# Four more x tiles of the first batch transposed by DMA in f16 halves instead of by TensorE

## The chip, the cores and the metric

The kernel runs on one core of one Trainium2 chip. The metric is the device time of one execution in microseconds (us). All times below are of that one core. The engines are TensorE (PE), VectorE (DVE), ScalarE (ACT), GpSimd (POOL) and SyncE (SP), which here only issues DMAs.

## The reference

```python
def reference(x, Wq, bq, Wk, bk, Wv, bv, Wo, bo, ffn_w, ffn_scale, ffn_bias):   # x: (8, 1024, 512) f32
    xn = layernorm(x)                                  # eps 1e-5
    q, k, v = (heads(xn @ W.T + b) for ...)            # 16 heads of 32
    scores = q @ k.T / sqrt(32)
    im = arange(1024) % 256
    scores = where(im[:, None] >= im[None, :], scores, -1e30)
    s = merge(softmax(scores) @ v) @ Wo.T + bo
    w = where(ffn_w >= 0, 1, -1)
    g = silu(clip((xn @ w.T) * ffn_scale + ffn_bias, -100, 100))
    return x + s * g
```

## The kernel before, in words

**Layout.** Each of the 8 batches has 1024 rows. They are cut into 8 tiles of 128 rows x 512 columns, so there are 64 tiles; tile i is tile i % 8 of batch i // 8. Every product needs the normalised x transposed: `xT[b % 2]` holds it as two f16 halves, a high one (`xTh`) and a low one (`xTl`, what rounding to f16 left over). A product with a weight runs three matmuls for each of 4 blocks of the contraction: high x high, high x low, low x high. The weights are split into the same two halves (`wh_*`, `wl_*`) by ACT and DVE.

**Two ways to transpose x.** Batch 0 takes the short way: PE transposes the f32 tile against an identity into a PSUM bank `pS` (`transpose_x` on PE, L491, semaphore `s_xt`). ACT copies the bank to `xTh` (`take_xt` on ACT, L725, `s_xh`), and DVE subtracts to make `xTl` (`take_xt` on DVE, L972, `s_xl`). The other batches split first: ACT writes the high half of tile i to `HL[k % 2]` (`split_x` on ACT, L717, `s_hi`), DVE writes the low half beside it (`split_x` on DVE, L965, `s_lo`), and SP issues one DMA transpose of both halves into `xT` (`transpose_x` on SP, L1231, semaphores `s_xd[k % 2]`). There are two `HL` buffers, so ACT's copy k waits until transpose k - 2 has landed.

**Where the first tiles lie.** x tiles 0 to 3 load into `xs`, 4 and 5 into `xr`, 6 and 7 into `On`. ACT normalises the even tiles and POOL the odd ones. The projection of Q and K of head group 0 comes as four products of 12 matmuls: (q, first half), (k, first half), (q, second half), (k, second half), called qk 0 to 3 below. The first two need tiles 0 to 3, the last two also tiles 4 to 7. ACT and DVE take each into `sg` (`stage_qk`, L735 and L981). Then copies from `sg` to `QK` follow by DMA: for each half six from SP (L1277) and six from ACT (`place_first`, L748). The V product of tile 0 (L535) follows on PE.

**What sets the order.** Nothing is scheduled at run time. Every engine merges its strands by due times in an abstract unit (`in_time`), and runs the merged list in order; an instruction that waits holds everything behind it on its engine. `wish` gives the due times of the x tiles, and `FIRST` = -84.67 is that of tile 0. `S_RING` hands out the three `pS` banks to score chunks and to the x tiles that PE transposes.

Two lists are timed by hand: `keep_busy` puts 36 matmuls with no use for the result in the first 16 us, 30 of them from the start and 6 behind the transpose of tile 3; `load_weights` on SP issues the loads of the weights as q0, k0, v, q1, k1, q2, k2 in the first 19 us.

Of the kernel before, what the change touches and what calls it, by code (L numbers as in the profile page):

```python
# [23 lines left out]
NSLOT = 6  # L24
NXS = 4
NPS = 3

# [110 lines left out]
def wish(kind, a, b):  # L138
    if kind == "x" and a == 0:
        return FIRST + (0.0, 0.11, 1.3, 1.35, 9.0, 9.23, 9.77, 9.91)[b]  # L140
    if kind == "x":
# [41 lines left out]
def past(kind, a, b=0):  # L183
# [6 lines left out]
S_RING = sorted([(at_s(i), "s", i) for i in range(len(S_TILES))] +  # L190
                [(wish("x", *divmod(i, NT)), "x", i) for i in range(NT)])
T_RING = sorted([(at_t(i), "t", i) for i in range(len(T_TILES))] + [(at_sums(n), "sm", n) for n in range(NU) if n not in ROW_AT])
# [72 lines left out]
def build(nc, x, wqT, wkT, wvT, woT, wfT, bqk_in, bvc_in, bo_in, fsc, fbi, idf, mqk, zrow, out):  # L265
    ctx = ExitStack()
    with ctx:
# [141 lines left out]
        def x_stands(b, t):  # L409

            if b == 0:
                return (s_xh, t + 1), (s_xl, t + 1)
            k = NT * (b - 1) + t
            return tuple((s_xd[j % 2], 16 * (j // 2 + 1)) for j in (k - 1, k) if j >= 0)
# [66 lines left out]
        def _(e):  # L481
# [9 lines left out]
            def transpose_x():  # L491
                for b in range(1):
                    for t in range(NT):
                        yield at("x", b, t)
                        i = b * NT + t
                        ln.wait_ge(s_id, 16)
                        ln.wait_ge(*row_done(i))
                        ln.wait_ge(*s_bank_free("x", i))
                        for c in range(4):
                            ins = e.transpose(s_bank("x", i)[:, c * P:(c + 1) * P],  # L500
                                              x_tile(i)[:, c * P:(c + 1) * P], identf[:, :])
                        ins.then_inc(s_xt, 1)
# [197 lines left out]
        def _(e):  # L700
# [16 lines left out]
            def split_x():  # L717
                for k in range(NTILE - NT):
                    i = NT + k
                    yield at("x", *divmod(i, NT)) - 1.9  # L720
# [4 lines left out]
            def take_xt():  # L725
                for b in range(1):
                    for t in range(NT):
                        yield past("x", b, t) + -0.02
# [80 lines left out]
            def take_outputs():  # L809
                for n in range(NU - 1):  # L810
                    yield at_pv(n, 4 * (n % NQS) + 3) + 0.59
                    if n < 2:
                        ln.wait_ge(s_xt, NT)
                    ln.wait_ge(s_oh, n - 1)
# [19 lines left out]
            def gates():  # L834
                for i in range(NTILE):
# [4 lines left out]
                    else:  # L840
                        ln.wait_ge(s_lo, NTILE - NT)
                        ln.wait_ge(s_f, i - NT + 1)
# [8 lines left out]
        def _(e):  # L851
# [113 lines left out]
            def split_x():  # L965
                for k in range(NTILE - NT):
                    i = NT + k
                    yield at("x", *divmod(i, NT)) - 0.83
                    ln.wait_ge(s_hi, k + 1)
                    e.tensor_tensor(HL[k % 2][:, 1, :], x_tile(i), HL[k % 2][:, 0, :], ALU.subtract).then_inc(s_lo, 1)  # L970

            def take_xt():  # L972
                for b in range(1):
                    for t in range(NT):
                        yield past("x", b, t) + 0.53
# [240 lines left out]
        def _(e):  # L1216
            ln = Line(e)

            def load_x():
                for i in range(NTILE):  # L1220
                    if i < NT:
                        yield (-119 if i < 4 else -117) + 0.1 * i
                    else:
# [3 lines left out]
                        else:  # L1227
                            ln.wait_ge(s_lo, i - NXS - NT + 1)
                    e.dma_start(x_tile(i), x_view[i // NT, i % NT]).then_inc(x_here(i)[0], 16)

            def transpose_x():  # L1231
                for k in range(NTILE - NT):
                    b, t = divmod(NT + k, NT)
                    yield at("x", b, t)
# [72 lines left out]
            def reload_x():  # L1307
                for i in range(NTILE - NT):
                    yield max(at("f", *divmod(i, NT)), past("o", *divmod(i - 2, NT)) + 3 if i > 1 else -99)
                    ln.wait_ge(s_xt, NT)  # L1310
                    ln.wait_ge(s_o[i % 2], 16 * (i // 2))
# [63 lines left out]
```

## Time and profile before

| | |
|---|---|
| median of 3 runs | 1741.29 us (1740.87, 1741.29, 1746.29) |
| the profiled execution, its own time | 1742.41 us |
| its span, first to last instruction | 1740.6 us |
| PE busy | 1676.8 us, 96% |
| DVE, ACT, POOL busy | 77%, 68%, 70% |
| granted TensorE clock, mean | 0.992 |

The span is what the trace can divide up; some 2 us of the execution's time lie around it. A clock of 1.00 is TensorE's full 2.4 GHz, 0.50 is 1.2 GHz. In the timeline the entries ACTq and SPq are DMA issues by the queue of that engine.

### The profile page before, as it was taken

What the parts mean: (1) busy time and instruction counts of PE and PEld (TensorE: products, weight loads), DVE (VectorE), ACT (ScalarE), POOL (GpSimd) and SP (SyncE); (2) the same over time, 40 slices, a digit from 0 to 9 for tenths busy, and PEclk for the clock granted to TensorE, in tenths of its full rate; (3) what the DMA queues carried; (4) which work ended last, traced back from release to release, by engine and by line L of the source; (5) the groups of instructions that cost most, each with busy time, mean ns of one, the idle gap of its engine ahead of it and who ended that gap; (6) DMA issues with size and microseconds to landing.
All of it is one profiled execution on the core that took longest, in us unless ns stands there. A gap on an engine that the chain in (4) does not pass through costs nothing.

```text
span 1740.6 us, 34003 instructions
## 1 busy us (share of the span) xinstructions
PE 1676.8 (96%) x11652; PEld 778.6 (45%) x11652; DVE 1342.8 (77%) x2620; ACT 1182.6 (68%) x2798; POOL 1222.8 (70%) x1210
## 2 busy tenths in 40 slices
PE   8989999999999999999999999999999999999978
PEld 3433444444444444444444444444444444444423
DVE  6888778787787976888777877778778787687872
ACT  4566777667667766677756777656777667667784
POOL 0077757786777768777588775888757786667773
PEclk9999999999999999999999999999999999999989
DMA  7313312243123421234122331224312242122111
GB/s 209 108 38 81 73 41 59 80 98 80 38 66 82 104 63 44 74 81 110 38 66 65 101 85 37 74 63 111 73 41 59 80 98 56 38 67 70 44 50 49
DMA packets 185038, 126.09 MB, mean 72 GB/s; under 512 B 106912, under 2 KB 159264, under 8 KB 184416
## 3 DMA queue, kind: packets, MB, share of 16 engines
q1 hardware_dynamic: 183904, 123.13, 28.2%
q8 instruction: 92, 1.51, 0.4%
q10 hardware_dynamic: 960, 0.79, 0.2%
q14 instruction: 82, 0.67, 0.1%
HBM read 41.50 MB, written 17.05 MB: 34 GB/s over the span
## 4 chain that ended last, share of the span: by engine, by line
PE 83%; ACT 10%; DVE 5%; issue 2%; ACTq 0%; DMA 0%; POOL 0%; SPq 0%; DVEq 0%
PE pJ L488 29%; PE pO L692 15%; PE pS L649 11%; PE pT L673 10%; ACT pS L802 4%; PE pT L669 3%; PE pJ L580 3%; PE pJ L581 3%; PE pJ L584 3%; PE pS L652 3%; ACT PT L790 2%; DVE mx L1002 2%; PE pT L633 2%; ACT acc L790 1%; ACT HL L723 1%
## 5 line engine op out<-in xcount | busy, mean ns | idle before, releaser
L1002 DVE TENSOR_REDUCE mx<-pS 128x1 f32<-128x512 f32 (+3 forms) x1216 | 782.7, 657 | 295.3 <-PE pS L649 178.3
L790 ACT ACTIVATE PT<-pT 128x512 f32<-128x512 f32 (+1 forms) x1092 | 630.3, 588 | 444.0 <-PE pT L673 362.0
L1178 POOL TENSOR_TENSOR acc<-acc,PT 128x512 f32<-128x512 f32 x620 | 762.1, 1262 | 34.4 <-PE pO L692 34.4
L649 PE MATMUL pS<-QK 96*128 96x512 f16 (+3 forms) x1280 | 392.1, 319 | 22.5 <-ACT pS L802 15.5
L673 PE MATMUL pT<-QK 97*128 97x512 f16 (+3 forms) x1280 | 393.6, 318 | 8.2 <-ACT acc L790 7.1
L802 ACT ACTIVATE pS<-pS,a 128x384 f32<-128x384 f32 (+3 forms) x512 | 270.8, 534 | 11.6 <-DVE a L1017 11.5
L692 PE MATMUL pO<-PT,V 128*32 128x512 f32 (+3 forms) x2824 | 264.7, 489 | 0.0
L649 PEld LDWEIGHTS pS<-QK 96*128 96x128 f16 x1280 | 124.1, 98 | 175.1 <-ACT pS L802 46.1
L488 PE MATMUL pJ<-xT,wh_q 128*128 128x512 f16 x512 | 191.0, 380 | 2.2 <-issue 1.7
L488 PE MATMUL pJ<-wh_v,xT 128*128 128x512 f16 x512 | 192.3, 378 | 0.6 <-ACT V L770 0.4
L488 PE MATMUL pJ<-xT,wh_k 128*128 128x512 f16 x512 | 192.7, 379 | 0.0
L652 PE MATMUL pS<-QK 128*128 128x128 f16 x1024 | 180.4, 220 | 11.3 <-DVE mx L1002 10.5
L669 PE MATMUL pT<-QK 128*128 128x128 f16 x1024 | 180.6, 220 | 8.5 <-ACT PT L790 5.7
L673 PEld LDWEIGHTS pT<-QK 97*128 97x128 f16 x1280 | 124.9, 98 | 120.3 <-ACT acc L790 12.6
L1188 POOL TENSOR_TENSOR On<-On,R 128x512 f32<-128x512 f32 x63 | 82.9, 1316 | 122.7 <-DVE R L1081 122.5
L1191 POOL TENSOR_TENSOR Onl<-On,Onh 128x512 f16<-128x512 f32 x63 | 73.2, 1162 | 105.1 <-ACT Onh L827 104.9
L488 PE MATMUL pJ<-wf,xT 128*128 128x512 fp8e4 x512 | 141.9, 378 | 0.0
L692 PEld LDWEIGHTS pO<-PT,V 128*32 128x32 f32 x2824 | 75.5, 110 | 136.6 <-issue 114.8
L669 PEld LDWEIGHTS pT<-QK 128*128 128x128 f16 x1024 | 91.3, 98 | 100.4 <-ACT PT L790 25.5
L652 PEld LDWEIGHTS pS<-QK 128*128 128x128 f16 x1024 | 94.7, 98 | 72.6 <-issue 12.3
L802 ACT ACTIVATION_READ_ACCUMULATOR pS<-pS,a 128x1 f32 x512 | 123.0, 240 | 0.0
L745 ACT ACTIVATE sg<-pJ,bqk 128x512 f16<-128x512 f32 x128 | 90.8, 709 | 45.9 <-PE pJ L488 41.1
(162 smaller groups left out, 2364.1 us busy)
## 6 DMA issues: line engine op xcount, KB each, us to landing
QK<-sg SPq DMA_DIRECT2D x756, 64.0 KB
xs<-in_x SPq DMA_DIRECT2D x60, 256.0 KB, 3.1
xr<-in_x SPq DMA_DIRECT2D x58, 256.0 KB, 3.0
out<-xr SPq DMA_DIRECT2D x58, 256.0 KB, 2.5
QK<-aT SPq DMA_DIRECT2D x256, 1.0 KB, 1.7
rq<-moved SPq DMA_DIRECT2D x132, 2.0 KB, 1.7
QK<-in_x SPq DMA_DIRECT2D x8, 256.0 KB, 3.8
QK<-in_mqk SPq DMA_DIRECT2D x2, 512.0 KB, 9.3
```

Of the source, the lines that this page charges most:

```text
L488: ins = e.matmul(bank(kind, a, b)[:, :], p, q, start=n == 0, stop=n == len(terms) - 1)
L649: ins = e.matmul(s_bank("s", i)[:, base:base + wide], q4[0:96, j, qc], k4[0:96, j, 0:wide], start=True, stop=True)
L652: ins = e.matmul(s_bank("s", i)[:, base + wide:base + width], q4[:, j, qc], k4[:, j, qc], start=True, stop=True)
L669: ins = e.matmul(slot[:, to:to + P], k4[:, j, kc], q4[:, j, q0:q0 + P], start=True, stop=True)
L673: ins = e.matmul(slot[:, to:to + 512 - q0], k4[0:97, j, kc], q4[0:97, j, q0:512], start=True, stop=True)
L692: ins = e.matmul(pO[32 * j:32 * j + 32, 512 - width:512], V[:, s, kb, 32 * j:32 * j + 32], probs, start=kb == 0, stop=kb == nkb - 1)
L745: e.activation(sg[:, 2 * which, cs], bank("qk", gn, o)[:, :], ACT.Identity, bias=bqk[:, which, gn % NG:gn % NG + 1]).then_inc(s_qh, 1)
L790: e.activation(probabilities_at(i), t_bank("t", i)[:, 0:cols], ACT.Exp, scale=SS).then_inc(s_p, 1)
L802: ins = e.activation(scores, scores, ACT.Exp, bias=row_shift(i)[:, c:c + 1], scale=SS, accum_out=rS[:, ROW_AT[n] % 2, part, c:c + 1])
L1002: e.tensor_reduce(mx[:, par, part, :].rearrange("p (j q) -> p j q", q=4)[:, heads[0]:heads[-1] + 1, qi], s_bank("s", i)[:, 0:cols].rearran ...
L1178: e.tensor_tensor(a, a, PT[:, RING_AT[i] % NPT, 0:width * len(heads)].rearrange("p (j q) -> p j q", j=len(heads)), ALU.add).then_inc(s_ap, 1)
L1188: e.tensor_tensor(On[n % 2][:, :], On[n % 2][:, :], R[:, :], ALU.mult).then_inc(s_on, 1)
```

## The change

A new constant `NXP = 4` says how many tiles PE transposes. Tiles 4 to 7 leave the PE strand and the two `take_xt` strands, and enter the strands that split and transpose the other batches: `k` now counts from tile 4. Their due times move from 9.0 ... 9.91 after `FIRST` to 8.0 ... 10.0. Those who waited for all eight PE transposes (`s_xt`) wait for four halvings (`s_lo`).

```diff
+NXP = 4
...
     if kind == "x" and a == 0:
-        return FIRST + (0.0, 0.11, 1.3, 1.35, 9.0, 9.23, 9.77, 9.91)[b]
+        return FIRST + (0.0, 0.11, 1.3, 1.35, 8.0, 8.8, 9.2, 10.0)[b]
...
-                [(wish("x", *divmod(i, NT)), "x", i) for i in range(NT)])
+                [(wish("x", *divmod(i, NT)), "x", i) for i in range(NXP)])
...
         def x_stands(b, t):
-            if b == 0:
+            k = NT * b + t - NXP
+            if k < 0:
                 return (s_xh, t + 1), (s_xl, t + 1)
-            k = NT * (b - 1) + t
             return tuple((s_xd[j % 2], 16 * (j // 2 + 1)) for j in (k - 1, k) if j >= 0)
...
             def transpose_x():
                 for b in range(1):
-                    for t in range(NT):
+                    for t in range(NXP):
                         yield at("x", b, t)
...
             def split_x():
-                for k in range(NTILE - NT):
-                    i = NT + k
+                for k in range(NTILE - NXP):
+                    i = NXP + k
                     yield at("x", *divmod(i, NT)) - 1.9
                     ln.wait_ge(*row_done(i))
                     ln.wait_ge(s_xd[k % 2], 16 * (k // 2))
...
             def take_xt():
                 for b in range(1):
-                    for t in range(NT):
+                    for t in range(NXP):
...
                     if n < 2:
-                        ln.wait_ge(s_xt, NT)
+                        ln.wait_ge(s_lo, NT - NXP)
...
             def split_x():
-                for k in range(NTILE - NT):
-                    i = NT + k
+                for k in range(NTILE - NXP):
+                    i = NXP + k
                     yield at("x", *divmod(i, NT)) - 0.83
                     ln.wait_ge(s_hi, k + 1)
...
             def transpose_x():
-                for k in range(NTILE - NT):
-                    b, t = divmod(NT + k, NT)
+                for k in range(NTILE - NXP):
+                    b, t = divmod(NXP + k, NT)
                     yield at("x", b, t)
                     ln.wait_ge(s_lo, k + 1)
```

The other edits only shift counts by the same four tiles (`load_x`, `reload_x`, `gates`). Behind the places shown here the order of every engine is as before, but for the names of the `pS` banks.

On PE, between product qk 1 (the last matmul with `wl_k`, `wh_k`) and product qk 2 (`wh_q`), there stood before:

```order
L488 MATMUL pJ<-xT,wh_k 128x512
L500 MATMUL pS<-identf,xr 128x128 [waits s_ln]
L500 MATMUL pS<-identf,xr 128x128 [waits s_lz]
L500 MATMUL pS<-identf,On 128x128 [waits s_ln]
L500 MATMUL pS<-identf,On 128x128 [waits s_xl,s_lz]
L488 MATMUL pJ<-xT,wh_q 128x512 [waits s_ql,s_xl,s_xh]
```

and each of the four L500 rows is followed by three more of its kind. With the change there stands at the same place:

```order
L489 MATMUL pJ<-xT,wl_k 128x512
L489 MATMUL pJ<-xT,wh_k 128x512
L489 MATMUL pJ<-xT,wh_q 128x512 [waits s_ql,s_xd1,s_xd0]
L489 MATMUL pJ<-xT,wl_q 128x512
L489 MATMUL pJ<-xT,wh_q 128x512 x2
```

The 16 transposing matmuls are gone, and product qk 2 waits for the landing of the DMA transposes (`s_xd0`, `s_xd1`).

On ACT, from the normalising of tile 6 (`On<-On,ab`) on, there stood before:

```order
L714 ACTIVATE On<-On,ab 128x512 [waits s_la]
L745 ACTIVATE sg<-pJ,bqk 128x512 [waits s_qk]
L731 ACTIVATE xT<-pS 128x4x128 [waits s_xt] x2
L707 ACTIVATE wh_v<-PT 128x512 [waits s_wv]
L731 ACTIVATE xT<-pS 128x4x128 [waits s_xt] x2
L707 ACTIVATE wh_v<-PT 128x512 x3
L758 DMA QK<-sg 32x2x512 [waits s_ql,s_qh,s_mask0]
```

and with the change, from the row ahead of it on:

```order
L724 ACTIVATE HL<-xr 128x512 [waits s_ln]
L715 ACTIVATE On<-On,ab 128x512 [waits s_la]
L724 ACTIVATE HL<-xr 128x512 [waits s_lz]
L724 ACTIVATE HL<-On 128x512 [waits s_xd0,s_ln]
L724 ACTIVATE HL<-On 128x512 [waits s_xd1,s_lz]
L746 ACTIVATE sg<-pJ,bqk 128x512 [waits s_qk]
L708 ACTIVATE wh_v<-PT 128x512 [waits s_wv]
L708 ACTIVATE wh_v<-PT 128x512 x3
L759 DMA QK<-sg 32x2x512 [waits s_ql,s_qh,s_mask0]
```

Four copies into `HL` have taken the place of four copies out of PSUM, two of them wait for a DMA, and the staging of product qk 1 (`sg<-pJ,bqk`), the halving of `wh_v` and the six DMA issues now stand behind these waits. DVE has the same: its four subtractions into `HL` stand ahead of its part in the staging of qk 1.

On SP, behind the load of the last Q and K weights (`PT<-in_wkT`, called k2), there stood before:

```order
L1247 DMA PT<-in_wkT 128x4x256
L1277 DMA QK<-sg 32x2x512 [waits s_ql,s_qh,s_mask0]
L1277 DMA QK<-sg 32x2x512 x5
L1279 DMA QK<-in_zrow 1x2048
L1277 DMA QK<-sg 32x2x512 [waits s_ql,s_qh]
```

and with the change:

```order
L1248 DMA PT<-in_wkT 128x4x256
L1239 DMA_TRANSPOSE xT<-HL 128x8x128 [waits s_lo] x4
L1278 DMA QK<-sg 32x2x512 [waits s_ql,s_qh,s_mask0]
L1278 DMA QK<-sg 32x2x512 x5
L1280 DMA QK<-in_zrow 1x2048
```

Four transposes have come in, behind all the early loads and ahead of the copies from `sg` to `QK`.

## Rows read from the trace of the kernel before

**Rows 1.** The page: span, and the chain that ended last, by engine.

```profile
span 1740.6 us, 34003 instructions
PE 83%; ACT 10%; DVE 5%; issue 2%; ACTq 0%; DMA 0%; POOL 0%; SPq 0%; DVEq 0%
```

**Rows 2.** A stretch: busy PE, PEld, DVE, ACT, POOL; PEclk, DMA share, GB/s.

```profile
400.00:800.00 400.00, 393.26 (x2771) 184.40 (x2769) 313.19 (x596) 269.94 (x623) 306.50 (x304) 1.00 0.29 72
```

**Rows 3.** The chain of waits, 18 to 46 us: start, length, what.

```profile
20.30 0.81 ACT xr L714
...
22.43 0.75 DVE sg L988
...
26.27 5.35 PE pJ L488 x24
31.65 0.69 ACT sg L745
```

**Rows 4.** Timeline of PE: start us, us, engine line op tiles count [idle before].

```profile
21.14 0.38 PE L488 MATMUL pJ<-xT,wh_k 128*128 128x512 f16 x1
...
26.27 0.38 PE L488 MATMUL pJ<-xT,wh_q 128*128 128x512 f16 x1 [1.72 <-issue]
```

**Rows 5.** Timelines of POOL, of the DMA issues of ACT, and of SP.

```profile
21.11 0.77 POOL L1135 TENSOR_SCALAR On<-On,ab 128x512 f32<-128x512 f32 x1
...
33.21 4.12 ACTq L758 DMA_DIRECT2D QK<-sg  x6
...
11.84 4.14 SPq L1247 DMA_DIRECT2D acc<-in_wqT  x1
16.02 2.97 SPq L1247 DMA_DIRECT2D PT<-in_wkT  x1
```

**Rows 6.** L1238, the DMA transposes of the other batches, and their halvings: ns min/median/max.

```profile
L1238 SPq DMA_TRANSPOSE xT<-HL x56: 1230/1256/2361, 140.0 to 1445.7; - x56
DMA to landing us min/median/max: 3.0/3.3/5.5
...
L723 ACT ACTIVATE HL<-xs x56: 618/638/793, 137.8 to 1443.9; 128x512 f16<-128x512 f32 x56
...
L970 DVE TENSOR_TENSOR HL<-xs,HL x56: 676/1151/1775, 138.6 to 1445.0; 128x512 f16<-128x512 f32 x56
```

**Rows 7.** DMA issues from 11 to 19 us; the last number: us to landing.

```profile
acc<-in_wqT SPq DMA_DIRECT2D x1, 512.0 KB, 13.1
PT<-in_wkT SPq DMA_DIRECT2D x1, 512.0 KB, 11.4
```

**Rows 8.** Three stretches, columns as in group 2.

```profile
23.00:25.00 2.00, 0.63 (x4) 0.42 (x4) 2.00 (x5) 1.78 (x4) 0.00 (x0) 1.00 1.08 333
25.00:27.00 2.00, 0.73 (x4) 0.40 (x5) 2.00 (x4) 1.74 (x4) 0.00 (x0) 1.00 0.84 189
...
140.00:145.00 5.00, 4.75 (x28) 1.57 (x30) 3.54 (x8) 5.00 (x13) 1.15 (x1) 1.00 0.48 105
```

**Rows 9.** Timelines of PE and its weight loads: the start, and the longest gap.

```profile
1.48 0.15 PEld L510 LDWEIGHTS pO<-row 128*128 128x128 f16 x1 [0.28 <-issue]
1.91 0.15 PEld L510 LDWEIGHTS pO<-row 128*128 128x128 f16 x1 [0.28 <-issue]
...
4.45 4.42 PEld L510 LDWEIGHTS pO<-row 128*128 128x128 f16 x21 [0.26 <-issue]
...
126.05 0.39 PE L649 MATMUL pS<-QK 96*128 96x256 f16 x1 [4.35 <-ACT pS L802]
```

**Rows 10.** Two stretches behind that gap, columns as in group 2.

```profile
128.00:130.00 2.00, 2.00 (x15) 0.98 (x17) 1.34 (x4) 2.00 (x8) 0.00 (x0) 0.50 0.00 0
130.00:132.00 2.00, 2.00 (x20) 0.42 (x12) 0.38 (x2) 0.59 (x3) 0.00 (x0) 0.82 0.00 0
```

**Rows 11.** Timelines of DVE and of POOL ahead of that gap.

```profile
118.99 4.87 DVE L1037 TENSOR_TENSOR mx<-mx 128x16 f32<-128x16 f32 x1
...
104.28 19.55 POOL L1178 TENSOR_TENSOR acc<-acc,PT 128x512 f32<-128x512 f32 x16
```

More of the change, by code:

```diff
@@ L840, in gates @@
                     else:
-                        ln.wait_ge(s_lo, NTILE - NT)
+                        ln.wait_ge(s_lo, NTILE - NXP)
                         ln.wait_ge(s_f, i - NT + 1)
@@ L973, in take_xt @@
                 for b in range(1):
-                    for t in range(NT):
+                    for t in range(NXP):
                         yield past("x", b, t) + 0.53
@@ L1227, in load_x @@
                         else:
-                            ln.wait_ge(s_lo, i - NXS - NT + 1)
+                            ln.wait_ge(s_lo, i - NXS - NXP + 1)
                     e.dma_start(x_tile(i), x_view[i // NT, i % NT]).then_inc(x_here(i)[0], 16)
             def transpose_x():
-                for k in range(NTILE - NT):
-                    b, t = divmod(NT + k, NT)
+                for k in range(NTILE - NXP):
+                    b, t = divmod(NXP + k, NT)
                     yield at("x", b, t)
@@ L1309, in reload_x @@
                     yield max(at("f", *divmod(i, NT)), past("o", *divmod(i - 2, NT)) + 3 if i > 1 else -99)
-                    ln.wait_ge(s_xt, NT)
+                    ln.wait_ge(s_lo, NT - NXP)
                     ln.wait_ge(s_o[i % 2], 16 * (i // 2))
```

## The prediction

> **What bounds the kernel now.** I read the page first, for the span and the chain that ended last [rows 1]: PE makes 83% of that chain, ACT 10%, DVE 5%, and DMA rounds to nothing. Then a long stretch of the middle [rows 2]: there PE is busy 393 of 400 us, and the other engines keep up. So the middle is a chain of PE work without slack, and its order does not change. All of it depends on the first projections: nothing there is tied to a fixed time, for the loads of later tiles are issued by SP behind the copies of this very start. A delay of the start should therefore reach the end whole, and a gain too.
>
> So I read the start closely. The chain of waits [rows 3] runs from ACT's normalising of tile 4 (20.3 us) over ACT and DVE to product qk 2, which begins at 26.27 us; its 24 matmuls (qk 2 and 3) are on the chain, and then ACT's staging of qk 3. The timeline of PE [rows 4] shows the same from PE's side: qk 1 ends at 21.5, then come the 16 transposes, and qk 2 begins at 26.27. These transposes are PE work, but PE was waiting anyway; what counts is how soon tile 7 stands in `xT`. Call the start of qk 2 S. Before, S = 26.3.
>
> **What the change removes.** 16 small matmuls on PE and four ACT copies and four DVE subtractions out of PSUM. The PE work lies in a gap, so its removal gives nothing by itself. The ACT and DVE work is replaced one for one, by copies of about the same length. Gain: 0.
>
> **What it adds: the way of tile 7 to `xT`.** I walk it with the durations of the other batches' tiles [rows 6]: high half on ACT 0.62 (the shortest; nothing else runs then), low half on DVE 0.68 (the shortest, since POOL is idle after 21.9 [rows 5] and nothing can hold DVE up), 1.25 for SP to issue a transpose, 3.3 from issue to landing (3.0 to 5.5). I allow 0.05 us for each hand-over from engine to engine; this is an estimate from the 0.01 to 0.1 us between rows of the chain.
>
> - Tile 4 is normalised at 21.1 [rows 3]. High half to 21.8, low half to 22.6, issue at 22.65.
> - Tile 5: ACT normalises tile 6 in between (0.7), so the high half is done at 23.1, the low half at 23.9, issue at 23.95.
> - Tiles 6 and 7 need the two `HL` buffers again. ACT therefore waits until the transposes of tiles 4 and 5 have landed.
>
> When do these land? At 22.65 the queue of SP is not empty. The load q2 was issued at 11.84 and k2 at 16.02 [rows 5], and they land 13.1 and 11.4 us later [rows 7], at 24.9 and 27.4, in the order of issue. The stretches say the same: the DMA engines are fully taken until 25 at 333 GB/s, and still 0.84 until 27 [rows 8]. Both loads are 512 KB, which take 1.5 to 1.6 us at that rate, so without ACT's own copies, which now come later, k2 would be down at about 26.4. I take the transposes to queue behind it. What one costs the DMA engines I get from 140 to 145 us, where one transpose and one 256 KB load ran alone: 0.48 x 5 = 2.4 us of all engines, less 0.85 for the load (262 KB at 333 GB/s, times 1.08) leaves 1.55 [rows 8]. So tile 4 lands at 26.4 + 1.55 = 28.0 and tile 5 at 29.5.
>
> The Trainium skill, page DMA: Bandwidth & Descriptors, section Queues, rings and completion order, says that all DMAs issued by SP use one ring on each DMA engine and are consumed in ring order. By that rule the transposes queue behind k2, as I take them to; a quick landing in spite of the loads would speak against it.
>
> - Tile 6: high half 28.05 to 28.7, low half to 29.4, issue 29.45, landing 32.75.
> - Tile 7: high half 29.55 to 30.2, low half to 30.95, SP free again at 30.7, issue 31.0, landing 34.3.
>
> So S = 34.4, which is 8.1 us later than before.
>
> The Trainium skill has a rule that speaks louder against the change. Its page VectorE: DVE Perf Modes, section The three transpose paths, gives 1309 ns for one 128x128 block of 16-bit numbers by DMA against 390 ns on TensorE. A tile here has eight such blocks; one after another they would be 10.5 us, tile 5 would land at 34.4 and tile 7 at 46.4, and the total would be 22 us. The trace does not bear this out: 56 transposes of this very shape land in 3.3 us [rows 6], so I give it no chance.
>
> **What is queued behind the waits.** On ACT the staging of qk 1 stood at 21.7 and now comes behind the high half of tile 7, at 30.2; DVE's part comes at 31.0. Behind it on ACT stand the halving of `wh_v` (4 x 0.6) and six DMA issues, which took 4.1 us at the other half [rows 5]: 33.3 to 37.5. Next on ACT is the staging of qk 2, which PE finishes 2.75 us after S, at 37.2 or later. So this work fits below the wait and costs nothing; if tile 7 came earlier than about 32.5, it would be what is late next. SP's six copies of the first half come behind the last transpose, from 32.3, and have until some 10 us after S. After S everything repeats at the old distances: the staging of qk 3 at S + 5.4 [rows 3], then the six issues of ACT and the V products. No time is won back there.
>
> **What it adds: a cold TensorE.** PE now has nothing to do from 21.5 to 34.4, 12.9 us. In the trace a gap of 4.35 us ended at 126.05 [rows 9], and behind it the granted clock was 0.50, that is 1.2 GHz, until about 131.3: 0.50 from 128 to 130 and 0.82 from 130 to 132 [rows 10]. This was 5.2 us at half speed, a loss of 2.6 us. At the start of the program the weight loads follow each other in 0.43 us, twice the 0.21 of later, from 1.1 to 4.45 [rows 9]: 3.4 us, a loss of 1.7. I take the mean, 2.1 us. It falls on the 24 matmuls of qk 2 and 3, which are on the chain, so it counts whole.
>
> **The sum.** 8.1 + 2.1 = 10.2 us. The profiled execution had 1742.41 with a span of 1740.6; with the change it would have 1752.6. The median of the runs is 1.1 below that execution, so I predict 1741.3 + 10.2 = 1751.5.
>
> **Bounds.** Low: the transposes don't feel the loads. Tile 4 lands at 25.95, tile 5 at 27.25, tile 7 is issued at 28.75 and lands at 32.05: S + 5.8, and with the smaller loss of clock 7.5. High: k2 lands at 27.4 as before, tile 5 at 30.5, tile 7 is issued at 32.0, and meets the copies from `sg` of SP and ACT that follow on its heels, 5.5 us: 37.5. With the larger loss of clock this is 11.2 + 2.6 = 13.8.
>
> **The rivals.**
> - *No queue.* The low case. For it speaks that a transpose is made of small pieces which could slip in between; against it that the loads land in order. 1749 (5.8 + 2.1 = 7.9). Chance 0.14.
> - *Crowded landing.* The high case, 1755. For it speaks that transposes with other copies behind them took up to 5.5 us [rows 6]; against it that SP issues its copies only 1.25 us later and the DMA engines are otherwise empty by then. Chance 0.12.
> - *Not slower: the stall at 119 us goes.* DVE's small maximum (L1037) took 4.87 us there, and ended just when POOL's 16 additions, back to back since 104.28, were over at 123.83 [rows 11]. PE's gap of 4.35 us and the 2.6 us of clock hang on it, 7.0 us together. If POOL and DVE met otherwise after a shifted start, 10.2 - 7.0 = 3.2 would be left, 1744.5, no measurable change. It decides once DVE reaches L1037 between two of the additions instead of ahead of them. Against it: both engines are shifted by the same start, so they should meet as before. Chance 0.06.
>
> The Trainium skill, page SBUF — State Buffer, section Who interferes with whom, says that a DVE instruction with two inputs in SBUF and a GpSimd instruction that reads SBUF exclude each other; by that rule the stall is a matter of which issues first.
>
> **Chances and range.** The forecast has 0.65, its own range is 1749.5 to 1754; 0.03 is left for what I did not think of. A measurement of this kernel tells about 0.3%, 5.2 us, from no change. The forecast and the first two rivals all lie above 1746.5, that is 0.91 slower; the third rival and half of the rest give 0.07 for the same; 0.02 faster. The range has to hold 8 in 10: I reach from 1747.5, just below the low case, to 1757, above the high case.
>
> **What would show it.** The first matmul of qk 2 near 34.4, waiting for the DMA into `xT`. Transposes issued near 22.7, 24, 29.5 and 31; the first two land 4 to 6 us after their issue, the last two about 3.3. ACT waits for them ahead of its third copy into `HL`. PE's matmuls 0.43 us apart for 3 to 5 us behind S. The staging of qk 3 some 7.5 us after S, and every later row about 10 us later than before, the stall at L1037 included, with PE as busy as before in the middle. The forecast is wrong if S is right but the end moves by another amount (slack in the middle that I don't see), or if the transposes land in another time than their 56 fellows.

## The result, and the profile after

The changed kernel takes 1755.69 us (median of 4 runs, 1754.62 to 1758.49); the kernel before, on the same chip, 1743.79 (4 runs, 1740.87 to 1746.89). The ratio is 1.007, with a 95% interval of 1.0045 to 1.0096: slower, by 11.9 us in the medians, where 10.2 were forecast. The profiled execution took 1755.81 us, its span is 1754.0 and its mean granted clock 0.988.

First the page and a stretch of the middle, to set beside [rows 1, 2]:

```profile
span 1754.0 us, 33979 instructions
PE 81%; ACT 9%; DVE 5%; issue 2%; DMA 1%; SPq 1%; ACTq 0%; DVEq 0%
```

```profile
400.00:800.00 400.00, 394.46 (x2765) 184.60 (x2758) 310.53 (x590) 275.30 (x639) 300.01 (x289) 1.00 0.29 71
```

The middle is as full as it was: PE busy 394 of 400 us. What is new in the chain is 1% DMA. The chain of waits from 20 us on shows where it lies, as against [rows 3]:

```profile
20.11 0.82 ACT xr L715
...
22.84 0.70 DVE HL L971
23.54 0.16 SPq L1239
23.75 4.60 DMA xT<-HL
28.44 0.64 ACT HL L724
29.10 0.70 DVE HL L971
29.80 0.36 SPq L1239
30.21 4.19 DMA xT<-HL
...
34.49 8.05 PE pJ L489 x24
42.57 0.69 ACT sg L746
```

The normalising of tile 4 starts where it did (20.11, before 20.30). Then the end is set by tile 5's halves, its transpose, tile 7's halves in the buffer that this frees, and its transpose: two landings, 8.8 us together, stand on the path. Product qk 2 starts at 34.49 instead of 26.27, and its 24 matmuls take 8.05 us instead of 5.35. 8.2 + 2.7 = 10.9 us: the staging of the first V product, next on ACT, starts at 48.27 where it started at 37.37.

The two sides of the gap, in the timelines of PE (the number in brackets is idle time, with what ended it) and of SP:

```profile
20.95 0.38 PE L489 MATMUL pJ<-xT,wh_k 128*128 128x512 f16 x1
34.49 0.58 PE L489 MATMUL pJ<-xT,wh_q 128*128 128x512 f16 x1 [13.16 <-DMA xT<-HL]
```

```profile
16.05 2.66 SPq L1248 DMA_DIRECT2D PT<-in_wkT  x1
22.33 9.21 SPq L1239 DMA_TRANSPOSE xT<-HL  x4
```

The line of the four transposes, by source, and ACT's timeline, which shows what stands behind its two waits:

```profile
L1239 SPq DMA_TRANSPOSE xT<-HL x4: 1233/1355/2649, 22.3 to 30.2; - x4
...
DMA to landing us min/median/max: 3.2/4.4/5.1
```

```profile
27.55 0.63 ACT L724 ACTIVATE HL<-On 128x512 f16<-128x512 f32 x1 [4.75 <-DMA xT<-HL]
28.44 0.63 ACT L724 ACTIVATE HL<-On 128x512 f16<-128x512 f32 x1 [0.26 <-DMA xT<-HL]
28.97 0.67 ACT L746 ACTIVATE sg<-pJ,bqk 128x512 f16<-128x512 f32 x1
...
30.56 0.70 ACTq L759 DMA_DIRECT2D QK<-sg  x1
...
48.27 1.08 ACT L771 ACTIVATE V<-pJ 128x512 f32<-128x512 f32 x2 [3.97 <-PE pJ L489]
```

In order of tiles 4 to 7 the landings took 5.1, 4.6, 3.2 and 4.2 us from the issue. The first two are over at 27.45 and 28.35. The queue ahead of them is there: k2, issued at 16.05, needed 10.5 us to land, so it was down at 26.5.

The Trainium skill, page DMA: Bandwidth & Descriptors, section Queues, rings and completion order, has SP's DMAs consumed in ring order. By that rule, the trace agrees: the first transpose landed 0.9 us behind the load ahead of it, 5.1 us after its own issue. From the 1309 ns for one block of its page VectorE: DVE Perf Modes, section The three transpose paths, eight blocks one after another are estimated at 10.5 us. The trace does not agree with that: 3.2 us for the least disturbed tile.

The clock, in stretches (the third number from the end is the granted clock, then DMA share and GB/s):

```profile
23.00:25.00 2.00, 0.00 (x0) 0.00 (x0) 0.53 (x1) 0.00 (x0) 0.00 (x0) 1.00 1.77 315
25.00:27.00 2.00, 0.00 (x0) 0.00 (x0) 0.00 (x0) 0.00 (x0) 0.00 (x0) 0.83 0.75 124
27.00:29.00 2.00, 0.00 (x0) 0.00 (x0) 0.69 (x1) 1.19 (x3) 0.00 (x0) 0.50 0.48 108
...
37.00:39.00 2.00, 2.00 (x6) 0.73 (x5) 0.00 (x0) 0.00 (x0) 0.00 (x0) 0.50 0.03 5
39.00:41.00 2.00, 2.00 (x8) 0.78 (x7) 0.47 (x1) 0.69 (x1) 0.00 (x0) 0.75 0.00 0
41.00:43.00 2.00, 2.00 (x11) 0.88 (x9) 0.28 (x1) 0.43 (x1) 0.00 (x0) 1.00 0.00 0
```

With PE idle since 21.3, the clock fell to 1.2 GHz in the stretch from 25 to 27 us and came back in that from 39 to 41, some 5 us after PE had taken up work: 6 matmuls in 2 us, later 11. A mean of 0.75 from 39 to 41 puts its return at 40.0, 5.5 us after S, and the 2.7 us lost are half of that.

And the stall that the third rival spoke of, DVE's small maximum and PE's gap behind it, in the timelines of DVE, POOL and PE; compare [rows 9, 11]:

```profile
129.81 4.88 DVE L1038 TENSOR_TENSOR mx<-mx 128x16 f32<-128x16 f32 x1
```

```profile
115.10 19.56 POOL L1179 TENSOR_TENSOR acc<-acc,PT 128x512 f32<-128x512 f32 x16
```

```profile
136.87 0.40 PE L650 MATMUL pS<-QK 96*128 96x256 f16 x1 [4.36 <-ACT pS L803]
```

Each row stands 10.8 us later than before, and its lengths are the same. Downstream I follow the 63 rows in which ACT takes an attention output out of PSUM (`On<-pO`, L818, before L817), one per unit of work. After against before they are late by 10.86 us (the first, at 94.81), 11.3 (the third, at 146.57), 11.9 (at 614.14), 12.0 (at 1607.52). So what is lost by the first V product is whole at the end, with 1.1 more on the way. Only the last few rows scatter (+10.8 to +13.4). In the last 100 us the granted clock falls to 0.50 at other places in the two executions, which may be why.

### The profile page after: what moved, and what is told of

It is laid out like the page before. It is cut to its first block, busy times and chain, and to the rows that moved or that the text cites. A ratio compares the mean times of both kernels' runs of the same rounds, so it can differ in the third digit from the quotient of the medians.

```text
span 1754.0 us, 33979 instructions
## 1 busy us (share of the span) xinstructions
PE 1679.4 (96%) x11636; PEld 777.8 (44%) x11636; DVE 1343.5 (77%) x2620; ACT 1183.0 (67%) x2798; POOL 1224.2 (70%) x1210
## 3 DMA queue, kind: packets, MB, share of 16 engines
q1 hardware_dynamic: 188128, 124.18, 28.4%
## 4 chain that ended last, share of the span: by engine, by line
PE 81%; ACT 9%; DVE 5%; issue 2%; DMA 1%; SPq 1%; ACTq 0%; DVEq 0%
PE pJ L489 29%; PE pO L693 15%; PE pS L650 10%; PE pT L674 9%; ACT pS L803 3%; PE pT L670 3%; PE pJ L581 3%; PE pJ L582 3%; PE pJ L585 3%; PE pS L653 3%; ACT PT L791 2%; DVE mx L1003 2%; PE pT L634 1%; ACT acc L791 1%; ACT HL L724 1%
```

## The experiments

In the table S is the first useful matmul of qk 2, and V the staging of the first V product; the profiled execution of before has S 26.27, V 37.37. The next two columns say how late V and the take of the 21st output (600 us) are against that execution. L1038 is the length of the stalled maximum (also called L1037 or otherwise, by the kernel). The ratios stand for all runs, the other columns for one execution of each kernel.

| kernel | S | 24 matmuls | V late | 21st late | L1038 | ratio to before, 95% |
|---|---|---|---|---|---|---|
| changed | 34.49 | 8.05 | 10.9 | 11.9 | 4.88 | 1.0045 to 1.0096 |
| e1_warm | 34.66 | 5.35 | 8.4 | 5.6 | 1.07 | 1.0027 to 1.0047 |
| e2_delay | 34.39 | 5.35 | 8.1 | 4.2 | 1.07 | 1.0028 to 1.0064 |
| e3_four | 33.34 | 7.72 | 9.4 | 7.2 | 1.05 | 1.0027 to 1.0061 |
| e4_late | 31.73 | 7.32 | 7.2 | 7.8 | 4.87 | 1.0021 to 1.0047 |
| e5_apart | 32.70 | 7.59 | 8.7 | 8.6 | 4.87 | one run |
| e6_all | 29.85 | 5.34 | 3.3 | 0.1 | 1.06 | 1.0010 to 1.0034 |
| e7_reduce | 26.32 | 5.35 | 0.0 | -0.1 | moved | 0.9994 to 1.0016 |
| e8_six | 30.32 | 7.02 | 5.7 | 5.5 | 4.89 | one run |
| e10_pause_before | 26.88 | 5.35 | 0.6 | 0.8 | 4.88 | 0.9987 to 1.0005 |
| e11_pause_after | 34.44 | 7.44 | 10.2 | 10.3 | 4.87 | 1.0042 to 1.0067 |
| e12_gap_before | 26.05 | 5.36 | -0.2 | -3.9 | 1.07 | 0.9977 to 0.9997 |
| e13_gap_after | 34.47 | 6.68 | 9.5 | 6.0 | 1.08 | 1.0019 to 1.0037 |

**e1_warm: the changed kernel with PE kept busy in the gap.** 56 matmuls more whose result nobody uses.

```diff
-                for when, count in ((-200, 30), (at("x", 0, 3) + 0.1, 6)):
+                for when, count in ((-200, 30), (at("x", 0, 3) + 0.1, 6), (at("qk", 0, 2) - 0.01, 56)):
```

> The changed kernel with 56 matmuls of no use for the result put into PE's gap ahead of product qk 2 (some 12.1 us at 0.215 us each, the gap is 13.5). Theory (late tiles plus a cold TensorE): qk 2 still starts at 34.5 us, since the transposes decide it, but its 24 matmuls with qk 3 take 5.35 us in place of 8.05, the staging of qk 3 begins at 39.9 in place of 42.6, and the whole is 2.7 us below the changed kernel, some 9.2 above the one before. Rival (the clock costs nothing of its own, the loss is all waiting): time as the changed kernel, some 11.9 above the one before.

1751.62 us (10 runs) against 1744.92 (14). A stretch in the gap, and the chain of waits behind S:

```profile
27.00:29.00 2.00, 2.00 (x11) 0.88 (x9) 0.61 (x1) 1.05 (x2) 0.00 (x0) 1.00 0.60 132
```

```profile
34.66 5.35 PE pJ L489 x24
```

The clock stays at 2.4 GHz, the 24 matmuls take 5.35 us again, and V comes 2.54 us sooner. The cold TensorE is a cost of its own. But from 130 us on the profiled execution had made up nearly 3 us more, which no theory of the start explains: its L1038 took 1.07 us and not 4.88. The median is 6.7 us above before, where 9.2 had been expected.

**e2_delay: the kernel before, held up by as much.** It has all eight PE transposes, and 46 idle matmuls behind the last one.

```diff
-                for when, count in ((-200, 30), (at("x", 0, 3) + 0.1, 6)):
+                for when, count in ((-200, 30), (at("x", 0, 3) + 0.1, 6), (at("qk", 0, 2) - 0.01, 46)):
```

> The kernel before with 46 matmuls of no use for the result behind PE's last transpose (9.9 us), so that qk 2 starts at about 34.5 us while nothing else of the change is there: no DMA transpose, no cold TensorE. Theory (a delay of the start reaches the end whole): the take of the first outputs from pO on ACT is 8.2 us later than in the kernel before, and the whole is 8.2 us longer. Rival (the middle has slack and the loss comes from other effects of the change): clearly less than 8.2, say 3 to 5 us.

1754.04 us (4 runs: 1748.69 to 1754.63) against 1744.92: +9.1 for a delay of 8.1 (the interval, 1.0028 to 1.0064, is 4.9 to 11.2 us). A late start without any DMA transpose costs what it is late. The profiled execution was the 1748.69 one; its maximum took 1.07 us and its 21st output was late by 4.2 instead of 8.1.

**e3_four: four buffers.** Tiles 6 and 7 have their halves in `Onl`, which nothing else uses then, so that ACT waits for no landing. DVE and SP take the halves of these tiles from there too.

```diff
+        def halves(k):
+            return Onl[:, k - 2, :].rearrange("p (a d) -> p a d", a=2) if k in (2, 3) else HL[k % 2]
...
-                    ln.wait_ge(s_xd[k % 2], 16 * (k // 2))
-                    e.activation(HL[k % 2][:, 0, :], x_tile(i), ACT.Copy).then_inc(s_hi, 1)
+                    if k > 3:
+                        ln.wait_ge(s_xd[k % 2], 16 * (k // 2))
+                    e.activation(halves(k)[:, 0, :], x_tile(i), ACT.Copy).then_inc(s_hi, 1)
```

> The changed kernel with two more buffers for the halves (tiles 6 and 7 are split into memory that is free until the outputs come), so ACT doesn't wait for the first two transposes to land. Theory (the two buffers and the queue in front of the transposes make the chain): all four are issued by about 29 us and the last lands at 31 to 32, qk 2 starts there, 2.5 to 3.5 us sooner than in the changed kernel, and the whole is as much shorter, some 9 above the one before. Rival (the DMA engines, not the buffers, set the pace: the transposes pile up behind the loads and slow each other): qk 2 starts at 33.5 or later and the whole is within 1 us of the changed kernel.

1752.46 us (4 runs), 7.5 above before where some 9 had been expected. SP's timeline and the chain:

```profile
22.63 3.83 SPq L1243 DMA_TRANSPOSE xT<-HL  x2
26.50 3.19 SPq L1243 DMA_TRANSPOSE xT<-Onl  x2
```

```profile
27.88 5.37 DMA xT<-Onl
33.34 7.72 PE pJ L492 x24
```

The last transpose is issued at 27.88 us instead of 30.21, yet S comes only 1.15 us sooner, between the two expectations and nearer to the rival's 33.5. Without its wait ACT reaches its six small copies at 25.8, in the midst of the transposes, and the last of these takes 5.4 us to land. The buffers are a wait that can be taken away, but the landings behind it grow.

**e4_late: nothing queued ahead.** The loads q2 and k2 are issued behind the first copies from `sg`.

```diff
-                                   ("q2", -111), ("k2", -110.9), ("o", -41), ("f", -40)):
+                                   ("q2", -73.9), ("k2", -73.8), ("o", -41), ("f", -40)):
```

> The changed kernel with the loads q2 and k2 (512 KB each) issued by SP behind the first copies from sg to QK instead of at 12 to 19 us, so the transposes of tiles 4 and 5 meet a shorter queue. Theory (they stand behind the loads): tile 4 lands 3.2 to 3.7 us after its issue in place of 5.1, tile 5 3.5 in place of 4.6, qk 2 starts 1 to 2.5 us sooner than in the changed kernel, and the whole is as much shorter. Rival (a transpose takes its 4 to 5 us for another reason here, such as its first use or its neighbour): landings as before, 5.1 and 4.6, and no change of time.

1751.01 us (5 runs), 6.1 above before. The line of the transposes, and the chain:

```profile
DMA to landing us min/median/max: 3.1/3.2/3.3
```

```profile
23.73 3.13 DMA xT<-HL
...
28.38 3.26 DMA xT<-HL
31.73 7.32 PE pJ L489 x24
```

S comes 2.8 us sooner, more than the 1 to 2.5 expected: the landings fell from 5.1, 4.6, 3.2 and 4.2 to 3.3, 3.1, 3.2 and 3.3. Tile 5 lands 1.5 us sooner (26.86, before the edit 28.35). Another 0.9 is the last landing, 3.26 for 4.19: here the small copies start 0.7 us behind its issue, not 0.35. So not all of the 2.8 is the queue. This is the low case of the prediction made real (S + 5.8 there, + 5.5 here), and the loads ahead are the largest single part of the delay.

**e5_apart: the small copies wait for the last transpose.** ACT's and SP's copies from `sg` of the first half wait until tile 7 has landed (the diff shows ACT's part; SP's is the same).

```diff
                     ln.wait_ge(s_mask[0], 16)
+                    for signal in x_stands(0, 7):
+                        ln.wait_ge(*signal)
                     ln.wait_ge(s_qh, 2 * half + 2)
```

> The changed kernel, in which SP and ACT issue the copies of the first half from sg to QK only after all four transposes have landed. Theory (the last transpose took 4.2 us, against 3.2 for the one before it, because ACT's copies came 0.35 us behind it): the last lands in 3.2, qk 2 starts at 33.5 us in place of 34.5, and the take of V on ACT is 1.0 us sooner than in the changed kernel; the delayed copies are hidden. Rival (the 4.2 has another reason): qk 2 stays at 34.5.

1752.95 us in one run. The line of the transposes, and the chain:

```profile
DMA to landing us min/median/max: 3.1/3.5/4.3
```

```profile
29.48 3.13 DMA xT<-HL
32.70 7.59 PE pJ L489 x24
```

Tile 7 lands in 3.1 us instead of 4.2, which gives 1.0 of the 1.8 us by which S is sooner; the rest is that the first two landed sooner in this execution (4.3 and 3.8), which the edit does not touch. They did so with k2, which was down at 25.8 here and not at 26.5: the first transpose lands 0.9 us behind that load in all seven executions that have it ahead (changed, e1, e3, e5, e8, e11, e13). Copies beside a transpose do hold it up: 4.2 us also in e1, e11 and e13. But in e4_late they started 0.7 us behind the last issue and it landed in 3.3 us, in the changed kernel 0.35 us behind and it took 4.2; how near they must be stays open.

**e6_all: all four edits.** Four buffers, late loads, copies apart, and 36 idle matmuls in the gap. The diff shows the last and the second; the other two stand as in e3_four and e5_apart.

```diff
+                for when, count in ((-200, 30), (at("x", 0, 3) + 0.1, 6), (at("qk", 0, 2) - 0.01, 36)):
...
+                                   ("q2", -73.9), ("k2", -73.8), ("o", -41), ("f", -40)):
```

> The changed kernel with all that was found: two more buffers for the halves, q2 and k2 loaded late, the copies from sg to QK behind the last transpose, and 36 matmuls of no use for the result in PE's gap. Theory (even with every removable cost gone, four transposes of 1.25 us issue and 3.2 us landing behind the halving end later than PE's way): the last transpose lands at 29.5 to 30, qk 2 starts there, 3.5 us later than in the kernel before, and the whole is 3 to 4 us longer than before where the stall of DVE's small maximum is the same in both. Rival (the way by DMA is as good once its waits are gone): qk 2 at or below 27 us and no difference.

1748.3 us (10 runs, 1741.95 to 1751.28) against 1744.21 (23 runs): +4.1. The landings are 3.4, 3.3, 3.3 and 3.2 us, S is 29.85. What I had found to be removable is gone; 3.6 us of the way are left, and the medians show about as much (the profiled execution does not: it has the short stall, and is the fastest of the ten). The way by DMA is longer here than that over PE even with all this out of its way.

**e7_reduce: the stalled maximum in another form.** The kernel before, with the two-input maximum as a reduction of one input into a tensor of its own.

```diff
-                        e.tensor_tensor(mx[:, par, 0, :], mx[:, par, 0, :], mx[:, par, 1, :],
+                        e.tensor_reduce(mm[:, par, :], mx[:, par, :, :].rearrange("p t c -> p c t"), AX.X,
                                         ALU.max).then_inc(s_am, 1)
```

> The kernel before, in which DVE's small maximum (L1037) is a reduction with one input in place of a tensor_tensor with two, into a small tensor of its own; nothing else is changed. Theory (the 4.87 us at 119 us is DVE waiting for POOL, whose additions ran back to back, because both inputs lie in SBUF): the operation takes 0.2 us in every execution, the take of the outputs on ACT behind it is 4.0 us sooner, as in the two runs where the stall fell to 1.07 us, and the median is 3 to 4 us below the kernel before. Rival (the 4.87 us has another reason, such as the fetch of code): the operation still takes 1 to 5 us and the time is the same.

1744.26 us (12 runs) against 1744.21 (23): nothing. DVE's timeline says why:

```profile
118.96 0.18 DVE L1038 TENSOR_REDUCE mm<-mx 128x16 f32<-128x32 f32 x1
119.17 4.67 DVE L1042 TENSOR_SCALAR a<-mm 128x16 f16<-128x16 f32 x1
```

The reduction passes in 0.18 us, and the very next operation, a scaling of 16 numbers per partition with one input, takes over the wait, 4.67 us. The expectation fell: it is not the two-input form alone that waits for POOL. The addition that POOL had running, the 12th of its 16, shows that the reduction went through beside it:

```profile
118.74 1.26 POOL L1179 TENSOR_TENSOR acc<-acc,PT 128x512 f32<-128x512 f32 x1
```

**e8_six: PE transposes six tiles, DMA only two.** Product qk 2 also waits for the two more tiles of PE.

```diff
-NXP = 4
+NXP = 6
...
-        return FIRST + (0.0, 0.11, 1.3, 1.35, 8.0, 8.8, 9.2, 10.0)[b]
+        return FIRST + (0.0, 0.11, 1.3, 1.35, 9.0, 9.23, 9.2, 10.0)[b]
```

> Half of the change: PE transposes tiles 4 and 5 too, only 6 and 7 go by DMA, each with a free buffer. Theory: the two transposes are issued at about 23.5 and 25 us, stand behind k2 and land 4.5 us later, qk 2 starts at 29 to 30 us, 3 us later than before and 5 sooner than in the changed kernel, PE's gap is some 6 us and cold TensorE costs 1 to 2.7; the take of V on ACT comes 4 to 6 us later than before. Rival (each tile costs the same): half of the 8.2 us, qk 2 at 30.4, no sharp difference to the theory; a start of 33 or later would say that the waiting for landed buffers is not what makes the change slow.

1749.88 us in one run. The chain:

```profile
24.30 5.93 DMA xT<-HL
30.32 7.02 PE pJ L489 x24
```

SP issues the two transposes from 22.87 on. One round of landings is left instead of two, and half of the loss: S + 4.05 and 1.67 us of clock make V 5.7 us late. S is 30.32, so that the rival (each tile costs the same, 30.4) is not told from the theory (29 to 30). And the one round is the longest of all (4.9 and 5.9 us), with the queued load ahead and ACT's copies, from 24.2 on, beside it.

**e10_pause_before and e11_pause_after: a wait in POOL's additions.** It was meant to let DVE in. The shifts that its count 1 stands for are made at 72 us, long before, so it never held POOL: in their work the two kernels are those of before and after again.

```diff
                     ln.wait_ge(s_pv, units(n) + 1)
+                    if k == 16:
+                        ln.wait_ge(s_a16, 1)
```

> The kernel before with one wait added on POOL: its 17th addition, at 119.5 us, waits until DVE has made the shifts of unit 1, so that the back-to-back additions leave DVE a gap. Theory (DVE's 4.87 us at 119 us, and the 4.67 that moved to the next operation when the first was made a reduction, are DVE waiting for a gap of POOL): the small maximum takes at most 0.7 us, PE's gap of 4.35 us goes, the take of the outputs behind it is 4.0 us sooner, and the median is 2 to 4 us below the kernel before, less than 4 because some executions of the kernel before have the short stall anyway. Rival (POOL's loss of its place costs as much): stall gone, time the same or longer.

> The changed kernel with the same wait on POOL. The stall is then the same in both kernels and can't blur their difference. Theory (8.2 us later start of qk 2 and 2.7 of cold TensorE, passed on whole): 10.9 us above e10_pause_before at the take of V and at every take of the outputs up to 1600 us, and 10 to 12 us in the median. Rival (the middle takes part of it back, or adds to it beyond the first 140 us): below 9 or above 13.

1743.48 us (11 runs) against 1744.39 (15), and 1753.55 (5 runs). The stall was there in both (4.88 and 4.87 us), so this missed its aim. As a repetition of the main comparison it is worth having: e11 is late against e10 by 9.63 us at V, 9.68 at the first output, 9.75 at the third, 9.5 at the 21st, 9.77 at 1,596 us, and 10.07 in the medians. (S of e10 is 26.88; the clock was at 0.6 from 12 to 16 us of that execution, which may be why.)

**e12_gap_before and e13_gap_after: the wait for the right count.** The last four of POOL's additions now wait until DVE has made the second set of shifts, L1041.

```diff
+                    if k == 16:
+                        ln.wait_ge(s_a16, 2)
```

> As e10_pause_before, with the wait mended: the first wait was for the first of these shifts, which DVE makes at 72 us, so it never held POOL; now POOL's 17th addition waits for the second one, behind the stall at 119 us. Theory (the 4.87 us are DVE waiting for a gap between POOL's additions): the small maximum takes at most 1.1 us, POOL pauses some 0.7 us at 120, PE's gap of 4.35 us goes, the take of the outputs at 135.3 us comes 3.5 to 4.0 us sooner, and the median is 1.5 to 4 us below the kernel before (less than 4, because some executions of it have the short stall anyway). Rival (another reason for the 4.87): it stays, and POOL's pause adds its length.

> The changed kernel with the same wait. Theory: again a short maximum, and against e12_gap_before 10.9 us at the take of V and in the middle, 9.5 to 12 in the median. Rival (the stall at 119 us has part in the difference of the two kernels): the difference of the medians leaves that band.

In e12 the timelines of DVE, POOL and PE, and a stretch behind the place:

```profile
118.68 1.07 DVE L1037 TENSOR_TENSOR mx<-mx 128x16 f32<-128x16 f32 x1
```

```profile
103.96 15.76 POOL L1180 TENSOR_TENSOR acc<-acc,PT 128x512 f32<-128x512 f32 x12
120.04 3.85 POOL L1180 TENSOR_TENSOR acc<-acc,PT 128x384 f32<-128x384 f32 x4 [0.32 <-DVE a L1041]
```

```profile
122.72 0.28 PE L649 MATMUL pS<-QK 96*128 96x256 f16 x1 [1.34 <-ACT pS L802]
```

```profile
124.00:128.00 4.00, 3.07 (x31) 0.95 (x30) 3.97 (x9) 3.26 (x10) 0.00 (x0) 1.00 0.02 1
```

DVE's maximum ends with the addition that is running, PE's gap shrinks from 4.35 to 1.34 us, the clock does not fall, and the third output is taken at 131.30 instead of 135.32, 4.0 us sooner, of which 0.3 were there before the stall. The kernel takes 1741.59 us (11 runs) against 1744.14 (21), ratio 0.9977 to 0.9997: one added wait beats both kernels. Of the eleven profiled executions without it that have the maximum in its old form, four had the short stall anyway; seven elevenths of 3.7 us, 2.4, is my estimate for the medians, and they show 2.6.

Why 3.7 us and not the 7.0 that I had put on the stall? Part of the answer is the stretch above: behind the gap PE is busy only 3.07 of 4 us at full clock, and DVE 3.97, so PE has room there. But the slow clock is not free. e1_warm and e2_delay have the same short stall (1.07 us) and the same gap of PE (1.93 us), and differ in the clock behind it:

```profile
132.00:136.00 4.00, 3.96 (x21) 1.34 (x25) 3.80 (x9) 4.00 (x14) 0.13 (x1) 0.59 0.09 19
```

```profile
132.00:136.00 4.00, 3.66 (x35) 1.41 (x35) 3.96 (x9) 4.00 (x14) 0.00 (x0) 1.00 0.07 12
```

The first is e1, the second e2: PE works on 21 matmuls against 35, at a mean clock of 0.59 against 1.00. From the start of the maximum to the third output e1 takes 13.55 us and e2 12.38. That e1 has the change and e2 not is no reason: in e12 and e13, with the clock full in both, it is 12.62 and 12.63. So the slow clock, 3.4 us at half speed, cost 1.2 us there, and not the whole half, 1.7.

e13 takes 1749.98 us (11 runs), 5.7 below the changed kernel as it was first timed. Against e12 it is late by 9.75 us at V, 9.80 at the first output, 9.75 at the third, 9.94 at the 21st, 9.98 at 1,602 us. The medians are 8.4 apart, below the 9.5 to 12 expected, which was to speak for the rival, that the stall has part in the difference. The runs leave that open: those of e12 span 6.0 us and those of e13 4.6, and the two profiled executions, both with the short stall, are 9.98 apart. At V, too, 10.9 had been expected. The difference there is the clock: 6.68 us for the 24 matmuls in this execution, 7.44 in e11, 8.05 in the changed kernel, with S within 0.05 us in all three.

## Why the prediction was right

**The middle has no slack.** Right, and shown from three sides: e2_delay (8.1 us of pure delay, 8.0 at the first output, +9.1 in the medians), e11 against e10 (9.6 at V, 10.07 at the end), e13 against e12 (9.75 at V, 9.98 at 1,602 us).

**The removal gives nothing.** Right: PE had been waiting, and with the 16 matmuls gone it waits 13.16 us in one piece.

**The way of tile 7, 8.1 us.** Measured 8.2, but that it fits so well is luck: its terms were mis-sized and cancel. I had let a transpose take 1.55 us of all DMA engines behind k2; tile 4 landed 0.9 us behind it and tile 5 another 0.9 later, so ACT was free at 28.4 and not at 29.5. From there to the issue of tile 7 it took 1.8 us and not 1.45, since SP was still issuing tile 6. And I had given tile 7 the undisturbed 3.3 us, though the copies from ACT's queue started 0.35 us behind its issue: 4.2. This is the second rival, in a small size; e5_apart gives 1.0 us back. The issues near 22.3, 23.8, 28.9 and 30.2 stand against the 22.65, 23.95, 29.45 and 31.0 of the forecast.

**What the 8.2 us are made of.** Undone one at a time: the queued loads 2.8 (e4, of which 0.9 is that the copies came later beside the last transpose), the copies beside the last transpose 1.0 (e5), the two buffers 1.15 net (e3, where the crowding takes some back). With everything undone 3.6 stay (e6). These need not add up, since each changes what the others meet.

**The cold TensorE, 2.1 us.** Right in kind (e1_warm makes it vanish), too small in the profiled execution: 8.05 - 5.35 = 2.7. The range given, 1.7 to 2.6, was a little narrow on both sides: the same start gave 1.3 (e13), 2.1 (e11) and 2.7. S was the same within 0.05 us; what differs is when the clock comes back.

**Queued behind the waits, nothing.** Right: the staging of qk 1 came at 28.97, ACT's six issues ended at 34.7, and the staging of qk 2 was wanted at 39.81.

**The rival "not slower", 0.06.** Its mechanism is real, its condition and price were wrong. I had written that it is decided by whether DVE reaches L1037 between two additions or ahead of them, and that the stall was worth 7.0 us. In the profiled executions L1038 took about 4.88 us in before, the changed kernel, e4, e5, e8, e10 and e11, and about 1.07 in e1, e2, e3 and e6. How far the start was shifted does not sort them, nor does the moment: in all of them DVE begins 0.2 us after the 12th addition has begun. The short one ends with that addition. The long one ends with the whole row: before, at 123.86, POOL's additions at 123.83. The difference, 3.8, is the last four additions of POOL, which e12 shows apart (128x384, 3.85 us). What decides between the two stays open. The stall can go either way, in the changed kernel as in the one before, and is worth 2.8 to 4.0 us between the first and the third output, too little against 10.9 to make the change neutral. It is little of the reason why single runs of one kernel differ: the 21 runs of before beside e12 lie within 7.7 us, and the 11 of e12 itself, where the profiled execution has no long stall, still within 6.0.

**The sum.** 10.2 forecast, of which V shows 10.9 and the medians 11.9. The other 1.1 us creep in behind V in this one pair of executions (0.4 by 147 us, 0.8 by 388, 1.0 by 614), and not in e11 against e10; I did not find their cause. Two executions of one order drift as well: e10 against before goes from 0.5 at the first output to 1.0 at 1,596 us. The measured 1755.69 is inside the range and above the forecast's own 1749.5 to 1754, at the 1755 of the second rival. That is for the most part not the rival's doing: of the 4.2 us above 1751.5, 2.5 are the kernel before, 1743.79 in 4 runs where I had 1741.29 in 3, 1.1 came behind V, and 0.6 is the clock. Its own part, 0.9 at the last landing, is taken back by the earlier landing of tile 5.

## What to carry to other kernels

Moving work from an engine that was waiting at that point to the DMA queues saved nothing here and put the latency of the DMA on the path, once for every round that the buffers allow; count the landings in a row, and look at what is queued ahead of them and issued beside them, before the busy shares. Behind gaps of 4.35 and 13 us TensorE ran at half speed for 2.7 to 5.5 us; idle matmuls in the gap cured that, and it cost the whole half where TensorE set the pace behind the gap (S to V), and less where DVE was as busy (1.2 of 1.7 us at 133 us). And a small DVE operation that meets a row of POOL operations without a pause may wait for several of them: one pause in POOL at the right place was the only edit here that beat both kernels.

## What was unexpected of the hardware

- A DVE operation on 128x16 numbers that began 0.2 us into one of POOL's back-to-back additions took either 1.07 or 4.88 us in the same code: it ended with that addition, or with the last of the four behind it. It was so for a two-input maximum, and for a one-input scaling to f16 (4.67 us), while a one-input reduction passed in 0.18 us beside the same addition (e7_reduce). The Trainium skill, page SBUF — State Buffer, section Who interferes with whom, has a two-input DVE instruction contend with a GpSimd one that reads SBUF, counts `tensor_scalar` among those that can, and `tensor_reduce` on trn2 among those that never do. By that rule the maximum and the scaling wait and the reduction passes, as they do here. That the waiting one can be passed by four further additions is what these runs add.
- A DMA transpose of 128x1024 f16 landed in 3.1 to 3.4 us with no load ahead (e4_late, e6_all), in 3.8 to 5.1 with a 512 KB load ahead in the same queue, the first of them 0.9 us behind that load in each of seven executions, and in 4.0 to 5.9 with 64 KB copies of another queue beside it, if these started no later than 0.35 us behind its issue.
- After a gap of 13 us the same 24 matmuls took 6.68, 7.44 and 8.05 us in three executions, against 5.35 without the gap.
